# Layer 4 of a decoder kernel: which of a unit's eight weightings run on GpSimd

## The reference, cut to what matters

```python
logits = jnp.einsum('bhqd,bhkd->bhqk', q, k) / jnp.sqrt(dh)
logits = logits + (1.0 - mask)[:, None] * -1e9
attn = jax.nn.softmax(logits, axis=-1)
attn = attn * group_prob[:, None, :, :]
out = jnp.einsum('bhqk,bhkd->bhqd', attn, v)
```

## Time and profile before

| what | us |
|---|---|
| median of 3 runs | 1481.15 (1476.33 to 1482.58) |
| the profiled execution | 1482.27 |
| its span | 1480.5 |
| TensorE busy | 1385.4 (94%) |
| VectorE busy | 1005.5 (68%) |
| ScalarE busy | 860.4 (58%) |
| POOL busy | 557.7 (38%) |

### The profile page before, as it was taken

The page is one execution under the profiler, slowest core; times in us unless marked ns, Lnnn a source line. Parts: engine busy times, 40 slices in busy tenths (PEclk is TensorE's granted clock), DMA queues, the critical chain, the costliest instruction groups (busy, mean ns, idle before and its releaser), DMA issues. The chain is left out here.

```text
span 1480.5 us, 41639 instructions
## 1 busy us (share of the span) xinstructions
PE 1385.4 (94%) x17414; PEld 970.7 (66%) x17414; DVE 1005.5 (68%) x2141; ACT 860.4 (58%) x1402; POOL 557.7 (38%) x727
## 2 busy tenths in 40 slices
PE   8999999999989999999999999988999899768997
PEld 5676656666656767667776676754655555447997
DVE  4577777766785556466563544676679889857896
ACT  1355666667656555464554646445547677637764
POOL 4146775623331121232221211341324444542766
PEclk9799999999999999999999999989999999978999
DMA  8588787756360312301011010143767544116452
GB/s 157 90 148 179 145 166 132 123 106 84 58 84 3 44 27 35 46 10 44 21 27 45 3 51 9 48 103 86 128 163 125 107 87 68 38 35 213 146 176 68
DMA packets 100298, 126.94 MB, mean 86 GB/s; under 512 B 7900, under 2 KB 90099, under 8 KB 97552
## 3 DMA queue, kind: packets, MB, share of 16 engines
q1 hardware_dynamic: 96496, 118.84, 39.8%
q0 software_dynamic: 2032, 4.24, 0.8%
q10 hardware_dynamic: 1584, 1.20, 0.3%
HBM read 51.10 MB, written 9.51 MB: 41 GB/s over the span
## 5 line engine op out<-in xcount | busy, mean ns | idle before, releaser
L975 ACT ACTIVATE probs<-eslot 128x1024 f32<-128x1024 f32 x188 | 192.5, 1024 | 105.7 <-PE eslot L706 102.6
L1200 DVE TENSOR_REDUCE mx<-mslot 128x4 f32<-128x1024 f32 x128 | 156.4, 1222 | 95.3 <-PE mslot L677 94.4
L1526 POOL TENSOR_SCALAR_AFFINE_SELECT probs<-probs 128x512 f32<-128x512 f32 x128 | 82.2, 644 | 331.5 <-ACT probs L973 331.2
L677 PE MATMUL mslot<-stack 48*128 48x256 f32 (+2 forms) x1110 | 165.7, 335 | 13.6 <-DVE mx L1200 7.1
L677 PEld LDWEIGHTS mslot<-stack 48*128 48x128 f32 (+1 forms) x1110 | 99.0, 189 | 100.8 <-issue 77.8
L1194 DVE TENSOR_REDUCE mx_blocks<-mslot 128x3 f32<-128x384 f32 x214 | 114.7, 554 | 57.6 <-PE mslot L677 41.2
L973 ACT ACTIVATE probs<-eslot 128x512 f32<-128x512 f32 (+1 forms) x256 | 111.6, 490 | 44.4 <-PE eslot L706 43.8
L706 PE MATMUL eslot<-stack 50*128 50x256 f32 (+1 forms) x1264 | 125.9, 276 | 7.0 <-ACT probs L975 3.6
L1465 POOL TENSOR_SCALAR ave<-amv 128x2 f32<-128x2 f32 x64 | 23.5, 367 | 288.4 <-DVE amv L1112 246.9
L721 PE MATMUL bank<-probs,v 128*32 128x256 f32 (+1 forms) x2048 | 125.7, 364 | 1.8 <-POOL probs L1526 1.0
L518 PE MATMUL bank<-slot_rows_sb,l 128*32 128x256 f32 x2048 | 113.8, 380 | 0.0
(11 more groups left out here) (277 smaller groups left out, 3375.9 us busy)
## 6 DMA issues: line engine op xcount, KB each, us to landing
stack<-split SPq DMA_DIRECT2D x192, 256.0 KB
w<-in_w SPq DMA_DIRECT2D x16, 1024.0 KB, 6.3
stack<-split SPq DMA_DIRECT2D x96, 128.0 KB
slot_rows_sb<-in_proj SPq DMA_DIRECT2D x15, 256.0 KB, 4.8
slot_rows<-hTf SPq DMA_DIRECT2D x4, 650.0 KB, 5.0
slot_rows_sb<-slot_rows SPq DMA_DIRECT2D x4, 650.0 KB, 5.2
expert_rows<-slot_rows SPq DMA_DIRECT2D x8, 260.0 KB, 2.7
hT<-in_xT SPq DMA_DIRECT2D x8, 256.0 KB, 9.1
```

The source lines that it names most:

```text
L677: mm = pe.matmul(ps[:, first:first + m], queries(u, h, k)[:, qt * P:(qt + 1) * P], keys(u, h, k)[:, 0:m], start=clear, stop=clear or qt == ...
L975: e = act.activation(PR[:, k, :, :, :].rearrange("p a k q -> p (a k q)"), ps[:, :, :, :].rearrange("p a k q -> p (a k q)"), ACT.Exp, scale ...
L1200: dve.tensor_reduce(MX[:, :, :, p].rearrange("p q a -> p a q"), MSLOT[0][:, :, :].rearrange("p a (q k) -> p a q k", q=TT), AX.X, ALU.max)\
L1526: pool.affine_select(diagonal, diagonal, [[0, 2 * TT], [1, P]], ALU.is_ge, 0.0, base=0, channel_multiplier=-1)\
```

## The change

One tuple. It is read in `weighted` (which semaphore tells that a pair is weighted), in the steps "weight" of VectorE and of POOL (who does it), and in SyncE's step "group", which waits for the last weighting on POOL before it loads the next group matrix into the same buffer.

```diff
-POOL_WEIGHTS = (4,)
+POOL_WEIGHTS = (2, 5)
```

## The result

The changed kernel takes 1527.39 us (median of 4 runs, 1521.93 to 1532.17) against 1481.87 us before; the ratio is 1.0319 (95% interval 1.0291 to 1.0346), so 47 us slower. I had forecast 1516.9 us, 34.6 us slower. The profiled execution took 1532.2 us with a span of 1530.4. It is the slowest of the four, with a mean granted clock of 0.956; the fastest, 1521.9 us, had 0.969. So times are compared by the ratios of many executions, and a single trace shows where the time lies.

A forecast was written before the change was run, and what follows sets the result against it. In layer 4 TensorE and VectorE were both busy about 28 of 31 us, and POOL's queue order was to decide. 16.0 + 12.2 + 8.9 - 2.5 = 34.6 us on 1482.3 gave 1516.9 us, range 1500 to 1528.

The forecast's parts named there:

- Part 1: Layer 4, units 32 to 36: pair 5's POOL weighting waits behind the mask conversion, delaying exponentials and mix; 16.0 us slower.
- Part 2: Layer 4, units 32 to 37: pair 2's POOL weighting precedes the normalisation, so TensorE's turn waits; 12.2 us slower.
- Part 3: Layer 4: TensorE's clock falls behind the longer gaps before turns (6.4 us) and mixes (2.5 us); 8.9 us slower.
- Part 4: Layer 4: VectorE has fewer weightings and the maxima's parts no longer meet POOL's weighting; 2.5 us faster.
- everything paid: Every clock fall at 1.6 us, each conversion stretched by 0.4, no relief: 44.6 us slower, 1526.9 us; 12 in 100.
- rival of the other side: Pair 5's wait absent, normalisation's delay hidden, the maxima's 9.8 us returned: 1472.5 us; 5 in 100.

The follow-up runs named there:

- e4: Changed kernel, with TensorE multiplying unread products in its gaps before mix step 6 and the turns: 1510.04 us, ratio 1.0200 to the kernel before.
- e8: Kernel before, with unread TensorE products before the turns of units 33 to 37: 1477.06 us, ratio 0.9977.
- e6: Kernel before with an empty tuple, so no weighting on POOL and all eight on VectorE: 1476.34 us, ratio 0.9967.
- e1: Only pair 5 weighted on POOL, pair 2 on VectorE, against the changed kernel's two: 1503.35 us, ratio 1.0156 to the kernel before.
- e2: Only pair 2 weighted on POOL, pair 5 on VectorE, against the changed kernel's two: 1499.45 us, ratio 1.0129 to the kernel before.
- e5: Kernel before with only pair 5 on POOL and the mask conversion one place later, behind that weighting: 1481.65 us, ratio 1.0012.
- e7: Kernel before with pairs 4 and 6 on POOL, mask conversion and residual bias placed behind pair 6's weighting: 1483.41 us, ratio 1.0020.
- e10: Changed kernel with unread TensorE products only before the turns of units 32 to 37, none before mixes: 1511.91 us, ratio 1.0227 to the kernel before.
- e3: Changed kernel with the mask conversion and pair 2's weighting each one place later in POOL's queue: 1488.62 us, ratio 1.0048 to the kernel before.

## Why the prediction was wrong in size

The direction, the place and the mechanism of both waits were right; 34.6 us were forecast and 47 came. The range was 1500 to 1528: the median, 1527.4, is just inside it, and the ratio put on the first median, 1481.15, gives 1528.4, just past it. The step that failed is the size of the clock's term; the relief's term, which had the wrong mechanism, comes second. Of the 46.8 us in layer 4, 28.9 are waits, 14.4 falls of the clock, and 3.5 stand in other stretches. Step by step:

- **Part 1, pair 5 behind the conversion: 16.0 us.** The wait without the clock is, by the stretches of e4, 3.6 us in each of the five units, 18.0. I had used the conversion's 1.20 us for unit 35 although its own row had 1.62; it is 1.46 in the changed kernel. Small, and in the rival.
- **Part 2, pair 2 ahead of the normalisation: 12.2 us.** The turns of e4 are 7.7 us longer than before's; before's include two falls of 1.6, so 10.9. With part 1, 28.9 us of waiting against 28.2 forecast. These two terms hold, and so do their parts, 2.45 us for the normalisation without its neighbour and 2.36 for the weighting. By turn, from unit 32 to 37, the same sum gives 3.0, 0.3, 1.5, 1.5, 1.6 and 2.9 against 3.2, 1.5, 1.7, 1.7, 1.7 and 2.4 forecast: unit 33's was wrong. That the two parts together miss by only 0.7 us is partly luck: the first is 2.0 too low, the second 1.3 too high.
- **Part 3, the clock: 8.9 us. This is the step that failed.** "1.6 us a fall" was read from one pair of stretches, whose fall lasted 3.4 us. Behind gaps of 3.1 to 3.3 us falls of 6.8 us came as well, and cost up to 3.1 us (the stretch of unit 36). Of the 17.6 us that e4 won, about 3 belong to the two falls before (e8); the new ones cost some 14. The turns were priced at 6.4 and the mixes at 2.5; the changed kernel against e4 has 12.8, of which 3.2 were old (1.6 each), and 4.8: 14.4 of new cost. That is the upper end that I had in the text; that it is the same to the tenth is luck, since it was nine falls at 1.6. The two turns that had a fall before (units 33 and 37) I left out, and theirs grew to 6.8 us.
- **Part 4, the relief: -2.5 us.** It has no place in the measured sum. The waits for maxima did fall by 3.9 us, and the maxima's parts lost their block, yet e6 shows the kernel faster with all weightings on VectorE. Why the 3.9 us don't show isn't settled; that TensorE waits for something else in the same stretches is argued, not shown. One thing that eats relief the traces do show: another short instruction of VectorE is blocked in place of the parts, twice in the changed kernel. By the rule of the Trainium skill (SBUF — State Buffer, "Who interferes with whom") I had written 0 for this term and 1519.4 us, nearer, but still 8 us short. That `one_hot` would run into POOL's weighting came true in two of the eight units. At 1350.57 TensorE waited 1.53 us for it, and unit 39's pair 7 came 1.6 us later after pair 6. This is 1.6 of the 3.5 us that no term of the sum had; for the rest no cause is shown.

So the rival "everything paid", 1526.9 us, comes nearest to what happened, with 12 in 100 from me; its added 2.0 us for the conversions is what Part 1 lacked. The rival of the other side is refuted by e1 and e2; its clause, that part 1 goes if the weighting isn't behind the conversion, is confirmed by e5, though its gain didn't come there.

## What to carry to other kernels

Before an operation is given to an engine with idle time, read what that engine's idle time waits for: here POOL was idle 62% of the span, but where the change put work its queue stood before a conversion or a normalisation was waited for. Two weightings a unit of 2.4 us cost 47 us there, and 3 us at other places. Even there (e7) they brought no gain, and short instructions of VectorE waited for them. Price a new stall of TensorE with the clock behind it, and take for it the longest fall seen for such a gap, not one pair of stretches. Here the tuple that says who does the work had to be tuned together with the order of the queue, and the case with nothing on the slow engine was faster than all others without the added products: it belongs among the candidates.

## What the runs showed of the hardware

- The granted clock fell to 0.50 at most gaps of TensorE of 2.6 us or more in layer 4, for 3.4 or 6.8 us, but not at one of 2.95 us in e2 (unit 32's turn), one of 3.11 in e1 and one of 2.82 in e10. Behind the three gaps of 1.43 us of the kernel before it stayed at 1.00, but it fell behind one of 1.60 us in e1, 1.53 in e3 and 1.33 in e5. So for like gaps both a fall and its length vary, and the length of the gap alone doesn't tell.
- Products that nobody reads, in the gaps, took the falls away: 17.6 us in the changed kernel (e4).
- A weighting of 128x1024 takes 2.33 to 2.39 us on POOL whatever its place, and on average 1.23 on VectorE. Two normalising instructions on POOL take 2.45 us undisturbed and 3.49 with a VectorE weighting between them.
- A short VectorE instruction that starts just behind a POOL weighting takes 1.5 to 2.4 us instead of 0.17 or 0.18: L1330 in the changed kernel, L1327 and L1330 in e5, L1345 in e7. With no weighting on POOL (e6) none in layer 4 did.
